# Gates' product moved behind the first key product, and eleven more TensorE fillers, in a gated cross-attention block

## The reference

```python
x = x + tanh(g_xattn) * attention(layernorm(x), ctx, ctx, mask)   # q, k go through W1,b1 and then W2,b2; v is ctx itself
x = x + tanh(g_ffn) * ffn(layernorm(x))                            # 128 -> 512 -> relu -> 128, all values rounded to fixed point
```

## Time and profile before

| | us |
|---|---|
| median of 3 runs | 68.75 (68.66 to 68.77) |
| the profiled execution | 68.81 |
| its span, first to last instruction | 67.0 |
| busy in the span: PE / DVE / ACT / POOL | 60.1 / 55.6 / 49.1 / 45.4 |

### The profile page before, as it was taken

The page is one execution under the profiler, slowest core; times in us unless marked ns, Lnnn a source line. Parts: engine busy times, 40 slices in busy tenths (PEclk is TensorE's granted clock), DMA queues, the critical chain, the costliest instruction groups (busy, mean ns, idle before and its releaser), DMA issues.

```text
span 67.0 us, 1864 instructions
## 1 busy us (share of the span) xinstructions
PE 60.1 (90%) x542; PEld 48.2 (72%) x546; DVE 55.6 (83%) x313; ACT 49.1 (73%) x139; POOL 45.4 (68%) x97
## 2 busy tenths in 40 slices
PE   4999999978999999689999999899999999888730
PEld 4989964746779888369968788879879788465410
DVE  4578894069969999999999999999989698989740
ACT  2603153539896798999999999999999996667500
POOL 5947589904799608899996899998953866851000
PEclk9999999999999999999999999999999999999999
DMA  0999999999940000000003000022300400340432
GB/s 0 277 398 389 400 408 397 416 418 406 416 189 8 0 0 0 5 0 5 15 0 117 0 0 0 0 79 87 125 32 0 156 15 34 122 156 7 154 117 78
DMA packets 3324, 9.09 MB, mean 136 GB/s; under 512 B 369, under 2 KB 754, under 8 KB 3314
## 3 DMA queue, kind: packets, MB, share of 16 engines
q1 hardware_dynamic: 3312, 8.98, 34.9%
q10 hardware_dynamic: 2, 0.00, 0.0%
HBM read 6.88 MB, written 2.10 MB: 134 GB/s over the span
## 4 chain that ended last, share of the span: by engine, by line
PE 54%; DVE 27%; issue 7%; ACT 4%; POOL 4%; DVEq 0%; POOLq 0%
PE bank_H L439 9%; PE bank_S L497 8%; PE bank_T L473 8%; DVE load_sb L726 7%; DVE st L659 6%; PE bank_O L554 5%; PE bank_A L513 5%; DVE h L753 4%; PE bank_H L539 4%; PE bank_T L488 4%; PE bank_A L506 3%; DVE sc L714 3%; POOL rs L383 3%; ACT pr L618 2%; DVE mv L662 2%
## 5 line engine op out<-in xcount | busy, mean ns | idle before, releaser
L642 ACT ACTIVATE h<-bank_H,fb_q 128x512 int8<-128x512 f32 (+2 forms) x28 | 17.2, 661 | 2.9 <-PE bank_H L539 1.8
L659 DVE BATCH_NORM_STATS2 st<-load_sb 128x6 f32<-128x128 f32 x64 | 14.0, 278 | 1.1 <-DMA load_sb<-in_packed 1.0
L383 POOL TENSOR_TENSOR rs<-ve,half 128x3 f32<-128x3 f32 (+5 forms) x9 | 10.5, 1166 | 5.0 <-DVE nm L667 4.9
L407 POOL TENSOR_SCALAR xq<-load_sb,nm,rs 128x128 int8<-128x128 f32 x28 | 12.3, 453 | 0.6 <-POOL rs L383 0.2
L618 ACT ACTIVATE pr<-sc,mn 128x120 f32<-128x120 f32 x32 | 12.2, 392 | 0.0
L497 PEld LDWEIGHTS bank_S<-kpT,xaT 128*128 128x128 f32 x64 | 9.0, 204 | 2.9 <-issue 2.1
L726 DVE SCALAR_TENSOR_TENSOR load_sb<-bank_A,gated_rec,load_sb 128x128 f32<-128x128 f32 x32 | 9.1, 342 | 1.8 <-POOL gated_rec L389 1.0
L397 POOL TENSOR_SCALAR xn<-load_sb,nm,rs 128x128 f32<-128x128 f32 x22 | 9.6, 446 | 0.3
L554 PE MATMUL bank_O<-w_q,h 128*128 128x128 bf16 x128 | 9.5, 220 | 0.4
L714 DVE CUSTOM_DVE_ANT_0 sc<-bank_S,mask_neg 128x120 f32<-128x120 f32 x32 | 7.1, 275 | 3.1 <-PE bank_S L497 3.0
L513 PE MATMUL bank_A<-load_sb,prT 120*128 120x128 f32 x64 | 9.2, 284 | 0.4 <-ACT prT L625 0.2
(11 more groups left out here) (81 smaller groups left out, 102.2 us busy)
## 6 DMA issues: line engine op xcount, KB each, us to landing
load_sb<-in_packed SPq DMA_DIRECT2D x6, 496.0 KB, 8.4
out_y<-y_sb SPq DMA_DIRECT2D x6, 256.0 KB, 2.0
load_sb<-in_packed SPq DMA_DIRECT2D x2, 512.0 KB, 10.7
load_sb<-in_packed SPq DMA_DIRECT2D x1, 576.0 KB, 13.5
load_sb<-in_packed SPq DMA_DIRECT2D x1, 514.0 KB, 7.0
load_sb<-in_packed SPq DMA_DIRECT2D x1, 448.0 KB, 6.2
load_sb<-in_packed SPq DMA_DIRECT2D x1, 432.0 KB, 12.1
load_sb<-in_packed SPq DMA_DIRECT2D x1, 428.0 KB, 12.7
```

What stands on the lines that cost most here:

```text
L383: nc.gpsimd.tensor_tensor(rs[:, at], ve[:, at], half[:, 0:at.stop - at.start], ALU.pow).then_inc(rs2_done, 1)
L407: nc.gpsimd.tensor_scalar(low_byte(xq16[g % RING], tile(j)), x_of(g, j), nm2[:, of(g, j, 1)], rs[:, roots(2, g, j)], ALU.add, ALU.mult).th ...
L642: nc.scalar.activation(low_byte(h16[g % RING], hcols(c, g)), bank_H[c][:, cols(g)], ACT.Relu, bias=fb1_q[:, c:c + 1]).then_inc(h_act[c], 1)
L659: nc.vector.bn_stats(st[:, START[g] + j, :], x_of(g, j)).then_inc(st_done, 1)
```

## The change

Two numbers of the fillers and one due number are changed. `spread_gates` goes from behind `fold_mm1` to the place between `project_keys(0)` (775) and `project_keys(1)` (838). `keep_warm0`, ahead of `fold_mm1`, has 15 fillers for 10, and `keep_warm1`, between `fold_mm1` and `fold_mm2`, has 34 for 28. No other engine's order changes.

```diff
-    spread_gates=[415],
+    spread_gates=[776],
...
-FILLERS = [10, 28, 2, 7, 4]
+FILLERS = [15, 34, 2, 7, 4]
```

## The result

| | before | changed |
|---|---|---|
| median, us | 68.76 (68.66 to 68.98, 4 runs) | 66.04 (65.94 to 66.51, 4 runs) |
| profiled execution / its span | 68.81 / 67.0 | 66.00 / 64.2 |

The ratio is 0.9614, with a 95% interval of 0.9562 to 0.9666. So the change is worth 2.7 us in the median, but not every execution got faster.

What follows compares the result with a forecast made beforehand. DVE's steady pipeline was taken to hang on its first row maximum, delayed by PE's queue. Moving it from 13.94 to 10.85 gains 3.1 us: 68.81 - 3.1 = 65.7; against the median 65.65, with 0.15 for small waits 65.8; range 65.2 to 69.4.

Steps and rivals of the forecast that it cites:

- The bound: 0 to 14 us: PE's queue delays DVE's first row maximum at 13.94; moving that moves the end by about as much.
- The first fold product: PE, ahead of the fold: five more fillers cost 0.29 us, so it starts at 4.23 instead of 3.94.
- The second fold products: PE, behind the 34 fillers: start at 6.93 instead of 6.81 at the low clock; +0.1 taken.
- the rise: TensorE's step from 1.2 to 2.4 GHz, read at about 13.7 us before; forecast has the stage fast from 6.9 us.
- The gates' product: PE, behind group 0's key product: costs 0.3 us at the high clock, 0.52 up to 0.75 at the low.
- The chain at the high clock: PE from 6.93 us: first key product ends 8.85, gates' product 9.15, second key product 9.95, six scores 10.75.
- The limit of the 514 KB load: DVE: load lands at 9.57, casts follow; first row maximum not before 10.72, 10.85 taken; time no better than 65.5.
- small waits: Allowance of 0.15 us for waits the prediction could not name, added to 65.65 to give 65.8.
- a rise that wanders: Clock step differing between runs, so times spread; prediction held three times of before within 0.11 us to speak against it.
- The middle case: Rival: clock step mid-stage, at 8.5 to 11 us; 67.4 with it at 10.4, covering 66.7 to 68.6; chance 0.11.
- The slower rival: Fillers don't raise the clock; moved product paid at the low clock, 0.64, giving 69.4; chance 0.28.
- Its last branch: Moved product breaks PE's run behind 9.34, clock step up to 2 us later: +0.7 beside +0.64, 70.1.

Runs made afterwards that it cites:

- the late casts: Changed kernel with VectorE's casts of the second weights behind the first row maxima and GpSimd's part later too: 66.76, 65.91, 66.28, 66.01 us.
- the moved product alone: Changed kernel with the 10 and 28 fillers of the kernel before, only the gates' product moved: median 65.72 us, against 68.51 of before.
- the fillers alone: Changed kernel with the gates' product back at its old place, the eleven added fillers kept: 65.63, 68.96, 65.77, 67.33 us.
- the product later still: Changed kernel with the gates' product behind the key product of group 2 and the scores of group 1: 66.41, 66.16, 65.98, 66.38 us.
- the moved product in the last set: Repeat, in the last of three sets, of the changed kernel with 10 and 28 fillers: median 66.06 us, against 68.44 of before.
- the variant with 10 and 20 fillers: Changed kernel, gates' product at its new place, with 10 and 20 fillers for 15 and 34: median 65.77 us, against 65.98 of the changed kernel.
- 10 and 34 fillers: Changed kernel, gates' product at its new place, without the five added fillers ahead of the fold: 65.73, 65.89, 65.86, 69.36 us.
- 15 and 28: Changed kernel, gates' product at its new place, without the six added fillers inside the fold: 66.02, 65.86, 65.72, 65.91 us.
- both places empty: Changed kernel with 0 and 0 fillers ahead of and inside the fold: median 68.72 us with the gates' product at its new place, 67.54 at its old.

## Why the prediction was right, point by point

**The bound** was read rightly. DVE's wait for the first scores, 3.05 us in front of 13.94, was the price, and its end moved by 3.08; the span moved by 2.8.

**The first fold product** moved from 3.94 to 4.21, +0.27 for a forecast of +0.29.

**The second fold products** were put at 6.93 at the latest, at the low clock. They came at 6.33, because the rise fell inside the 34 fillers: 1.46 us where 1.98 was the sum at the low clock. The variant with the late casts, in which the rise came only at the end of the fillers, has them at 6.88: the low-clock sum was right, the place of the rise was not. The prediction had named the earlier rise as the rule of the Trainium skill ("TensorE: Matmul & The Clock Gate", Part 1), with a time no better than 65.5 for it, and both came true: the best execution of the changed kernel took 65.81.

**The gates' product** behind the first key product costs 8.97 - 8.66 = 0.31 on PE at the high clock (forecast 0.3), and 0.75 at the low one (forecast 0.52 to 0.75).

**The chain at the high clock.** Scores were forecast to end at 10.75; the six start at 9.88 and last 0.82, 10.70. The first key product started at 7.86 instead of 8.25, but the key products hold PE for 0.80 and 0.91 where 0.6 and 0.8 were forecast, so the scores end only 0.05 ahead of the forecast.

**The limit of the 514 KB load.** First row maximum at 10.85 forecast, 10.86 measured. The instant is right, the reason only in part. The load landed at 2.57 + 7.1 = 9.67 and the casts began at 9.65, as forecast. But the row maximum follows the end of the scores by 0.16, here (10.70 to 10.86) as in the kernel before (12.30 + 1.48 = 13.78 to 13.94), and so it does in seven of the ten profiles with an early rise, among them that of the moved product alone: there PE was 0.26 us earlier with its scores, and the row maximum was too, 10.60. So in the changed kernel it was still PE that released DVE. The casts bound it in the other three (the fillers alone, the product later still, the moved product in the last set), 0.34 to 0.46 behind the scores, and in two of these they had waited for the load:

```profile
9.77 0.70 DVE L768 TENSOR_SCALAR mp<-load_sb 128x1028 int8<-128x1028 f32 x1 [0.20 <-DMA load_sb<-in_packed]
```

In that one the row maximum came 1.08 behind the start of the casts; in the changed kernel this would have been 10.73, so the scores held DVE for 0.13 more. The forecast left out the 0.16 behind the scores and so took the load for the limit; with it the scores would have stood at 10.91, within 0.1 of that limit. That the value came out to 0.01 is luck. Nor is 10.72 a firm bound: the load took 6.1 to 7.3 us in the nine profiles with a rise up to 6.0, and in four of them the row maximum came earlier, at 10.60 to 10.69.

**What the 0.3 us between 3.08 and 2.8 was.** The prediction kept 0.15 for small waits. One place where it may have gone is a tiny operation of DVE beside GpSimd's normalisation of six tiles, 0.45 us instead of 0.17 (DVE's timeline, changed kernel):

```profile
18.27 0.45 DVE L667 TENSOR_SCALAR nm<-mv 128x3 f32<-128x3 f32 x1
```

The same operation took 0.17 in the variant with 10 and 20 fillers. Why it was stretched wasn't tested.

**What was wrong,** besides the limit of the load, was one step in the rivals: "the three times of before lie within 0.11 us, which speaks against a rise that wanders". It does wander. The rise lies before 3.9 us with 10 and 34 fillers and with 10 and 20, near 5.5 in the first profile of the changed kernel and near 5.0 in its second, near 6.0 with 15 and 28, at 6.9 with the late casts, and at some 13.7 in the profile of before; and 6 of the 29 timed executions of the kernel before have 65.3 to 65.6 us. Three close times were three draws of the likelier kind. The Trainium skill says in the same Part that the point of the transition differs between runs of one kernel, and gives ±500 ns; the runs here agree that it differs, but by far more, 3.7 to 6.9 us among the early ones alone. The prediction had given that case only 0.11. The middle case itself, a rise in the middle of the stage, occurred, by the times, in no execution of the changed kernel; values of 66.93 and 67.33, as it would give, occurred only where the product breaks the stretch; neither was profiled.

So the mechanism was right and its form was not: the change doesn't turn a kernel that stays slow into a fast one, it turns an early rise in about one execution of five into one in nearly all. The executions of before that have it, by their times, are with 65.3 to 65.6 some 0.5 us faster than the median of the changed kernel. The five fillers with their later start of the fold, and the product between the two key products, are the candidates; what each takes was not separated.

The slower rival (fillers don't raise the clock) is refuted: in the profile with 10 and 20 PE ran nothing but fillers before the first fast product, and with both places empty no execution of eight has the early rise. Its price for the moved product, 0.64, was near the 0.75 measured. Its last branch, in which the product breaks the run behind 9.34 and delays the rise further, didn't occur where it could be seen: with both places empty and the product at 10.05 the rise came near 12.6, among the scores.

What stays open is why an early break costs so much. Behind it PE in the kernel before works from 5.18 to the late rise at 13.7 with no idle time in the timeline, longer than the changed kernel needs from 0.92 to 5.5. The prediction counts the one-column product at 7.40 as a second break; it stood in its place in every run, so this wasn't tested. Nor was it tested whether a product of another kind in the gates' place would do the same.

## What to carry to other kernels

Where a kernel's first microseconds hang on TensorE's clock, start its queue with one unbroken stretch of matmuls, and put anything that interrupts it (a wait, a product of two columns) behind that stretch, even if it then stands on the critical path: 0.3 us at the high clock bought 3 us here. The stretch need not reach the first long product: up to 5.1 us was enough in six of six. Fillers that don't bring the rise are a loss, 0.9 us here. And time such a change in ten executions or more: three equal times don't exclude a second kind of execution, and a profile shows only one of them.

## What was not expected of the hardware

- The same program, on one chip in one set of runs, takes either 65.3 to 65.6 or 68.2 to 69.0 us. The profiles of the variants, where the rise lies anywhere between some 3.7 and 6.9 us or at 12 to 14 us, say by what: PE's durations for the same shape halve at another time. That a fast execution of the kernel before has the early rise is inferred from its time; none was profiled.
- A break of 0.5 us in the stretch (two matmuls of two columns, with their weight loads) goes with the loss of the early rise, by the times, in 30 of 39 executions, whether it stands at 3.4 us or behind the first fold product (4.7 and 4.9). A gap of 0.71 us at 5.1 lost it in none of six.
- The granted clock of the profile reads 1.00 on both sides of the step. Only durations show it: 0.80 and 0.49 for the pair of 128x128, 1.57 and 0.87 for that of 128x360.
